# First attention of a two-layer block: head pairs on two halves of the array's rows, stacks sent through memory, small pieces of work between score rounds

## The chip, the cores and the metric

The kernel runs on one core of a Trainium2 chip. The metric is the device time of one execution in microseconds. A core has a matrix engine (PE, with weight loads shown as PEld), a vector engine (DVE), a scalar engine (ACT), a general engine (POOL), and a queue that issues transfers (SP). Each works through its own list in order and waits on semaphores for the others. PE works out of SBUF into PSUM banks of 512 fp32 columns.

## What is computed

The block takes x of 16 batches of 512 tokens of 128 features: layer norm, first attention times a gate made from a quantised FFN, residual, layer norm, second attention times a gate from a mixture of experts, residual. The change touches the first attention alone, which has 16 heads of 8 dimensions:

```python
Q = relu(x @ Wq + bq); K = relu(x @ Wk + bk); V = relu(x @ Wv + bv)   # x: [16, 512, 128]
scores = einsum('bqhd,bkhd->bhqk', Qh, Kh) / sqrt(8)
scores = where(key_mask == 0, NEG, scores)
scores = where(tril == 0, NEG, scores)
attn = softmax(scores) * query_mask
out = einsum('bhqk,bkhd->bqhd', attn, Vh) + x
return gamma * (out - mean) / sqrt(var + 1e-8) + beta
```

## The kernel before, in words

Five stages run one after another: `norm_exact`, `ffn`, `attention0` (the first attention), `attention1` (the second), `experts`. `attention0` treats a **unit** of one batch and 8 heads at a time, so there are 32 units and two make a batch. The loop `turns` runs over two batches (four units, `s` = 0 to 3); each engine has its own `turn` with the order of its work written out by hand.

**Exact scores from bf16.** Q and K are projected in fp32 on PE (`project`, L1070), and ACT writes them twice, fp32 (`F`, L879) and bf16 (`part`, L880). POOL's `split` (L815 to L817) makes the two remaining bf16 parts. For a head, six products of parts are summed at once by laying the parts under each other in the rows of the stacks `QS` and `KS`: 6 x 8 rows, a row with the key mask at 64 and three rows with the bf16 parts of the negated row maximum at 96 (`MROW`). A matmul on the stacks uses 96 rows for maxima and 99 for scores. SP fills the stacks from `part` with 12 transfers of 64 KB for Q (L730) and 12 for K (L730), one mask row for each half of the heads (L735) and three rows of maxima a unit (L740). Four sets of stacks are in use.

**Unit.** For each pair of heads there are four banks of maxima (`max_bank`, L1082 and L1084): Q as weights, K as moving columns, and an added block of -1e30 above the diagonal, with the 128 x 128 matrices `identb` and `far`. DVE reduces each bank pair (L948). All 16 banks of unit u+1 are made while unit u is scored; DVE then splits the maxima into three bf16 parts (`m_split`, L956 to L959), PE turns them (`turn_m`, L1136), ACT copies them out (L898) and SP puts them into `QS`. For each pair there are also five score banks (`score_bank`, L1095 with `add_far`, L624 or L627), keys on partitions, into two alternating PSUM banks `pST`; ACT takes the exponential of each bank (L887). `weigh` (L1123) multiplies by V, four heads on four column groups, in fp32; ACT copies the result (`o_evac`, L892), PE turns it back (`turn_o`, L1130) and DVE divides by the sums (`o_normal`, L984 to L989).

**What sets the order.** `both` mixes maximum banks into the five score banks of a pair:

```python
for k in range(5):
    for _ in range(-(-len(todo) // (5 - k))):
        max_bank(u + 1, *todo.pop(0), i1)
    score_bank(u, p, k, i)
    if k in after:
        after[k]()
```

Pairs 0 and 1 carry five maximum banks each, pair 2 six, pair 3 none. PE begins unit u after `m_put` (the maxima's rows have landed), and its first bank is a maximum bank that also needs the stacks. In even units SP issues the stacks of the next batch (`stacks_q`, `stacks_k`), then `m_rows`, then the second half of the K stacks. At the end of an even unit DVE runs `normalise` (L995 to L998) and then `v_evac` (L965 to L973, nine instructions: bias, ReLU, key mask, ones columns). At the end of an odd unit it runs `normalise_x1` (to L1009). POOL's `residual` (L838 to L841) stands between them.

`attention1`, which is not changed, already works on pairs of 64-row heads (L1646, L1653 for scores, L1663 for maxima) with one pair of score banks and an exponential of 1024 columns (L1456).

Of the kernel before, what the change touches and what calls it, by code (L numbers as in the profile page):

```python
# [629 lines left out]
def attention0(nc, NB, XN, G, KM, ident, identb, far, x, Wq, bq, Wk, bk, Wv, bv, gamma, beta, x1_d, mask_d):  # L630

# [10 lines left out]
    PARTS_Q = (0, 0, 0, 1, 1, 2)  # L642
    PARTS_K = (0, 1, 2, 0, 1, 0)
    MASK, MROW = 64, 96
    VC = DH + 1
    PER_D, PER_G = 112, 20
    STACK = 7 * 16
    with ExitStack() as c:
# [7 lines left out]
        rows = sb("rows", [P, 3, P])  # L656
        xst = sb("xn_staged", [P, TOK])
# [4 lines left out]
        QS = [sb(f"QS{i}", [P, UH, TOK], BF16) for i in range(4)]  # L662
        KS = [sb(f"KS{i}", [P, UH, TOK], BF16) for i in range(4)]
        V = [sb(f"V{i}", [P, TB, HEADS * VC + 32 - VC]) for i in range(2)]
        vtmp = sb("vtmp", [P, TB, P])
        PT = [sb(f"PT{i}", [P, 5, TOK]) for i in range(4)]
        MX = sb("max", [P, UH, TB])
        mrest = sb("mrest", [P, UH * TB])
        mp = sb("mparts", [P, 3, UH * TB], BF16)
        mT = sb("mT", [UH * TB, 3, P], BF16)  # L670
        OT = sb("OT", [P, TOK])
        den = sb("den", [P, TB, 4])
# [6 lines left out]
        pST = [ps(f"pST{i}", [P, TOK]) for i in range(2)]  # L679
# [5 lines left out]
        zeroed, ones_set, v_set = sem("k_zeroed"), sem("k_ones_set"), sem("v_set")  # L685
        q_zeroed, q_ones_set = sem("q_zeroed"), sem("q_ones_set")
# [8 lines left out]
        q_stacked, k_stacked = [sem(f"q_stacked{i}") for i in range(2)], [sem(f"k_stacked{i}") for i in range(2)]  # L695
# [8 lines left out]
        loads = 3 + 2 * 2 * DH + 3  # L704

        @block.sync
        def _(sp):
# [12 lines left out]
            sp.wait_ge(mask_made, 3)  # L720
            sp.dma_start(mask_d, part[0:NT, 1, 0, 0:P]).then_inc(mask_stored, 16)
            sp.wait_ge(mask_stored, 16)

# [4 lines left out]
            def stack(i0, half, n, S, order, stacked):  # L728
                for at, k in enumerate(order):
                    sp.dma_start(S[i0 + half][DH * at:DH * at + DH, :, :],  # L730
                                 part[64 * half:64 * half + 64, n, k, :]).then_inc(stacked[half], 16)

            def mask_row(b, i0, half):
                row = mask_d[bass.ds(b * TB, TB), :].rearrange("(o a t) p -> o a (t p)", o=1, a=1)
                sp.dma_start(KS[i0 + half][MASK:MASK + 1, :, :], row.to_broadcast([1, UH, TOK])).then_inc(k_stacked[half], 16)  # L735

            def m_rows(u, i):
                mT_in.wait(sp, u)
                for k in range(3):
                    sp.dma_start(QS[i][MROW + k:MROW + k + 1, :, :], mT[:, k, :]).then_inc(m_put, 16)  # L740

            def stacks_q(b, i0, last_reader=None):
                q_parts.wait(sp, b)
                if last_reader is not None:
                    st_ready.wait(sp, last_reader)
                for half in range(2):
                    stack(i0, half, 0, QS, PARTS_Q, q_stacked)

            def stacks_k(b, i0, half):
                k_parts.wait(sp, b)  # L750
                stack(i0, half, 1, KS, PARTS_K, k_stacked)
                mask_row(b, i0, half)

            stage(0)
            sp.wait_ge(q_ones_set, 2)
            sp.wait_ge(ones_set, 2)
            stacks_q(0, 0)
            stacks_k(0, 0, 0)
            stage(1)
            m_rows(0, 0)  # L760
            stacks_k(0, 0, 1)
# [8 lines left out]

            def turn(i, first, last):
                for s in range(4):
                    u, b = i * 4 + s, i * 2 + s // 2
                    prep = s % 2 == 0 and not (last and s == 2)
                    if s % 2 == 0 and not (first and s == 0):
                        load_x(b - 1)
                    if prep:
                        if first and s == 0:
                            sp.wait_ge(q_ones_set, 4)
                            sp.wait_ge(ones_set, 4)  # L780
                        stacks_q(b + 1, (s + 2) % 4, 20 * (u - 1) + 19)
                        stacks_k(b + 1, (s + 2) % 4, 0)
                    if not (last and s == 3):
                        m_rows(u + 1, (s + 1) % 4)
                    if prep:
                        stacks_k(b + 1, (s + 2) % 4, 1)
                    if s % 2 == 0 and not (first and s == 0):
                        store_x1(b - 1, (s // 2 + 1) % 2)
                    if s % 2 == 1 and not (last and s >= 1):
                        stage(b + 2)  # L790
# [6 lines left out]
        def _(g):  # L797
            def clear(i0):

                for S in KS[i0:i0 + 2]:  # L800
                    g.memset(S[:], 0.0).then_inc(zeroed, 1)
                g.wait_ge(zeroed, i0 + 2)
                for S in KS[i0:i0 + 2]:
                    g.memset(S[MROW:MROW + 3, :, :], 1.0).then_inc(ones_set, 1)
                g.wait_ge(ones_set, i0 + 2)

            clear(0)
            for t in V:
                g.memset(t[:], 0.0).then_inc(v_set, 1)
            g.wait_ge(v_set, 2)  # L810

            def split(step, b, n, filled, stacked, done):
# [7 lines left out]
            g.wait_ge(w_in, 16 * loads)  # L820

            for w, into in ((wq0, wq), (wk0, wk)):
                for half in range(2):
                    g.tensor_copy(into[:, 64 * half:64 * half + 64].rearrange("c (d h) -> c d h", h=UH),
                                  w[:, 64 * half:64 * half + 64].rearrange("c (h d) -> c d h", h=UH)).then_inc(w_ordered, 1)
            step = Steps(g, pool)
            split(step, 0, 0, q_in, q_stacked, q_parts)
            split(step, 0, 1, k_in, k_stacked, k_parts)
            clear(2)
            before = step.n  # L830

            def residual(step, b, parity):

# [9 lines left out]

            def turn(i, first, last):
# [4 lines left out]
                for s in (0, 2):  # L849
                    b = i * 2 + s // 2  # L850
                    if not (last and s == 2):
                        split(step, b + 1, 0, q_in, q_stacked, q_parts)
                        split(step, b + 1, 1, k_in, k_stacked, k_parts)
                    if not (first and s == 0):
# [1250 lines left out]
```

## Time and profile before

| | us |
|---|---|
| runs | 3512.64 median (3512.46, 3512.64, 3522.1) |
| profiled execution | 3512.28, its span 3510.6, mean granted clock 0.935 |
| PE busy in the span | 2817.1 (80%) |
| DVE busy | 2341.5 (67%) |
| ACT busy | 1521.8 (43%) |
| POOL busy | 1262.9 (36%) |

Times in the profile are microseconds from the span's start, unless marked ns. The granted clock is a share of TensorE's full 2.4 GHz, and it has two levels, 0.5 and 1.0; a value between them is a mean. Matmuls overlap, so the time that one costs is read from start to start and not from its length. In a row of the trace, "out<-in" names what is written and read, xN is how many were merged, and the brackets give the idle time of the engine before it and what ended that. "issue" there is a wait that the profile shows no releaser for.

### The profile page before, as it was taken

How to read it: one execution, taken by the hardware profiler on the slowest of the kernel's cores; microseconds unless marked ns; L12 is line 12 of the kernel's file. 1: busy time of each engine (PE TensorE's matmuls, PEld its weight loads, DVE VectorE, ACT ScalarE, POOL GpSimd, SP SyncE). 2: the span in 40 equal slices, each digit the busy share in tenths (PEclk: the TensorE clock that was granted, in tenths of full speed). 3: DMA queues.
4: the chain of work that ended last, by engine and by line, in shares of the span. 5: the costliest groups of instructions: out<-in, count | busy, mean ns of one | idle time of the engine just before them, and what ended most of it. 6: DMA issues, size and time to landing. Idle time of an engine off the chain costs nothing. (4 is left out here: it accounts for less than half of the span.)

```text
span 3510.6 us, 66700 instructions
## 1 busy us (share of the span) xinstructions
PE 2817.1 (80%) x21313; PEld 1947.4 (55%) x21313; DVE 2341.5 (67%) x5836; ACT 1521.8 (43%) x2623; POOL 1262.9 (36%) x1384
## 2 busy tenths in 40 slices
PE   0046367777777788499999999999999987999999
PEld 0024134444444444366666666666666656888888
DVE  8978657777776777466666666666666645555555
ACT  3434234454444455254555545555555532232232
POOL 4546602121211211155555555555555550000000
PEclk9986579998989899699999999999999998999999
DMA  1000123222221312101111111111111112010100
GB/s 48 0 6 0 25 30 47 39 44 35 41 45 36 51 35 32 37 28 35 34 34 34 34 34 34 34 34 34 34 34 34 32 35 64 24 36 24 34 26 24
DMA packets 152527, 116.24 MB, mean 33 GB/s; under 512 B 35506, under 2 KB 127155, under 8 KB 152372
## 3 DMA queue, kind: packets, MB, share of 16 engines
q1 hardware_dynamic: 152372, 114.25, 14.2%
q8 instruction: 87, 1.43, 0.2%
q14 instruction: 68, 0.56, 0.1%
HBM read 60.96 MB, written 17.32 MB: 22 GB/s over the span
## 5 line engine op out<-in xcount | busy, mean ns | idle before, releaser
L1539 DVE CUSTOM_DVE_ANT_0 a_scored<-a_pMax,a_causal 128x128 bf16<-128x128 f32 (+3 forms) x1024 | 449.7, 485 | 444.0 <-PE a_pMax L1663 444.0
L948 DVE TENSOR_REDUCE a_max<-a_pMax 128x2 f32<-128x256 f32 (+3 forms) x512 | 406.8, 822 | 209.3 <-PE a_pMax L1084 198.4
L887 ACT ACTIVATE a_PT<-a_pST 128x512 f32<-128x512 f32 x640 | 370.6, 597 | 403.3 <-PE a_pST L624 268.4
L1456 ACT ACTIVATE a_PT<-a_pST 128x1024 f32<-128x1024 f32 (+1 forms) x384 | 338.8, 882 | 361.2 <-PE a_pST L1653 349.8
L1082 PE MATMUL a_pMax<-a_KS,a_QS 96*128 96x128 bf16 (+3 forms) x1024 | 283.8, 329 | 203.3 <-DMA a_QS<-a_mT 134.6
L1405 POOL TENSOR_SCALAR_AFFINE_SELECT a_PT<-a_PT 128x256 f32<-128x256 f32 x512 | 203.0, 409 | 603.5 <-ACT a_PT L1456 573.0
L1942 ACT ACTIVATE m_silu<-m_pG 128x512 f32<-128x512 f32 x256 | 153.3, 599 | 410.2 <-PE m_pG L2034 410.2
L1671 PE MATMUL a_pO<-a_PT,a_V 128*64 128x512 f32 (+3 forms) x2048 | 307.3, 443 | 0.7 <-POOL a_PT L1405 0.7
L1082 PEld LDWEIGHTS a_pMax<-a_KS,a_QS 96*128 96x128 bf16 x1024 | 106.8, 105 | 309.4 <-issue 197.9
L1095 PE MATMUL a_pST<-a_QS,a_KS 99*128 99x512 bf16 (+3 forms) x1024 | 256.8, 315 | 16.4 <-ACT a_PT L887 14.4
L2042 PEld LDWEIGHTS m_pY<-m_w,m_hT 128*128 128x128 f32 x2048 | 248.0, 191 | 9.9
L815 POOL TENSOR_TENSOR a_rest<-a_qk,a_parts 128x512 f32<-128x512 f32 x32 | 37.0, 1155 | 593.9 <-ACT a_parts L880 593.7
L1989 DVE TENSOR_TENSOR m_hT<-m_pU,m_silu 128x512 f32<-128x512 f32 x256 | 177.0, 691 | 108.9 <-PE m_pU L2034 90.6
L2042 PE MATMUL m_pY<-m_w,m_hT 128*128 128x128 f32 x2048 | 248.8, 275 | 0.0
L1423 POOL TENSOR_TENSOR a_SM<-a_PT 128x768 f32<-128x768 f32 x128 | 235.0, 1836 | 10.6
L1671 PEld LDWEIGHTS a_pO<-a_PT,a_V 128*64 128x64 f32 x2048 | 136.6, 137 | 164.5 <-issue 145.3
L1910 POOL TENSOR_TENSOR m_out<-m_silu_acc,m_y 128x512 f32<-128x512 f32 x16 | 20.3, 1270 | 561.5 <-ACT m_silu_acc L1934 561.5
L1084 PE MATMUL a_pMax<-far,identb 128*128 128x128 bf16 x1024 | 221.9, 235 | 0.0
L2002 DVE SCALAR_TENSOR_TENSOR m_acc<-m_pY,m_cw,m_acc 128x128 f32<-128x128 f32 x448 | 126.3, 344 | 126.8 <-PE m_pY L2042 126.8
L1646 PE MATMUL a_pST<-a_q_high,a_k_high 64*128 64x512 f32 (+3 forms) x1024 | 198.9, 385 | 4.0 <-ACT a_PT L1456 4.0
L1653 PE MATMUL a_pST<-a_max_rows,a_ones_rows 64*128 64x512 f32 (+3 forms) x1024 | 151.8, 333 | 50.5 <-DMA a_max_rows<-a_mT 50.5
L1663 PE MATMUL a_pMax<-a_k_high,a_q_high 64*128 64x128 f32 (+3 forms) x1024 | 166.8, 363 | 8.0 <-DVE a_max L1539 6.6
(282 smaller groups left out, 6861.7 us busy)
## 6 DMA issues: line engine op xcount, KB each, us to landing
a_rden<-inverse_sums_dram SPq DMA_DIRECT2D x256, 128.0 KB, 2.9
a_QS<-a_parts SPq DMA_DIRECT2D x192, 64.0 KB
a_KS<-a_parts SPq DMA_DIRECT2D x192, 64.0 KB
a_xn_staged<-xn SPq DMA_DIRECT2D x32, 256.0 KB, 2.4
a_max_rows<-a_mT SPq DMA_DIRECT2D x512, 2.0 KB
ln_x<-in_L_attn_x SPq DMA_DIRECT2D x8, 512.0 KB, 7.2
a_x<-in_L_attn_x SPq DMA_DIRECT2D x16, 256.0 KB, 3.0
x_dram<-a_att SPq DMA_DIRECT2D x16, 256.0 KB, 3.8
```

The costliest lines, as they stand in the source:

```text
L887: a.activation(PT[p][:, k], pST[(5 * p + k) % 2][:], ACT.Exp, scale=SCALE).then_inc(exped.sem, 1)
L948: v.tensor_reduce(MX[:, 2 * p:2 * p + 2, j], pMax[j % 2][:, :, 0:(j + 1) * P], AX.X, ALU.max, negate=True).then_inc(maxed.sem, 1)
L1082: pe.matmul(pMax[j % 2][:, hh, 0:(j + 1) * P], QS[i][0:MROW, h, j * P:(j + 1) * P], KS[i][0:MROW, h, 0:(j + 1) * P], start=True, stop=False)
L1084: mm = pe.matmul(pMax[j % 2][:, hh, j * P:(j + 1) * P], identb[:], far[:], start=False, stop=True)
L1095: pe.matmul(bank[:, at:at + TOK - kb * P], KS[i][0:MROW + 3, h, kb * P:(kb + 1) * P], QS[i][0:MROW + 3, h, kb * P:TOK], start=(at == 0), s ...
L1405: g.affine_select(out=blocks, in_=blocks, compare_op=ALU.is_ge, fill=0.0, base=0, pattern=[[0, 2], [1, P]], channel_multiplier=-1).then_in ...
L1423: step.then(g.tensor_tensor(S[:, :, P:TOK], T[:, :, P:TOK], T[:, :, AT[1]:AT[1] + TOK - P], ALU.add))
L1456: a.activation(PT[s.q % 2][:, :, k * TOK:k * TOK + w], pST[:, :, 0:w], ACT.Exp, scale=SCALE).then_inc(exped.sem, 1)
L1539: last = v.tensor_tensor_reduce(scored[:, cc, at:at + w], pMax[:, cc, at:at + w], causal[:, TOK - w:], -1.0, 3e38, ALU.add, ALU.min, MX[pa ...
L1646: pe.matmul(pST[:, cc, at:at + w], K[i][rows, keys], Q[i][rows, queries], start=(n == 0 and at == 0), stop=False)
L1671: mm = pe.matmul(pO[DH * cc:DH * cc + DH, kb * P:TOK], V[pair // 2 % 2][:, kb, head:head + DH], PT[pair % 2][:, cc, AT[kb]:AT[kb] + TOK - ...
L2042: mm = pe.matmul(pY[e % 2][:, t], HT[HC * (e % 2) + k][:, t * P:(t + 1) * P], W2[:, e, k], start=(k == 0), stop=(k == HC - 1))
```

## The change

- **Pairs on row halves.** A pair is now head h of the first eight and head h of the second eight. One has rows 0 to 63 of the array, the other rows 64 to 127. The mask row moves to 48 and the maxima to 49 to 51 within each half, so there are two sets of stacks and not four. A unit is four such pairs.
- **Rounds.** A pair has three score rounds (1024, 1024 and 512 columns over both heads) into one pair of banks `pST`, and three maximum rounds into two alternating pairs of banks. Three exponentials replace five, 12 a unit.
- **Stacks through memory.** Q and K parts are written to DRAM (`put_q`, `put_k`, 3 and 4 transfers a batch), with copies made by repeated sources. From there each of two groups of four pairs is filled with four transfers of 4 KB rows (`stack`). The ones of the mask rows are set once. The three maxima's rows of both halves take 2 transfers a unit, not 3.
- **Ahead.** Maxima run 6 pairs ahead of scores (`LEAD`). Projections are made two batches ahead and put out in odd units, the values one batch ahead in even units.
- **Pieces.** PE's weighs, turns and projections, and DVE's layer norms, are cut into pieces and stand between the rounds. The values' evacuation goes from DVE (nine instructions) to ACT (one); the bias is added on PE by a one-row matmul, and the key mask is left to the scores. `turn_m` is one transpose and not three.

The core of the diff:

```diff
+    PAIRS, NS, NM, LEAD = 4, 3, 3, 6
+    AT = (0, TOK, 2 * TOK, TOK + 3 * P)
+    WIDTH = (TOK, TOK, 2 * P)
+    ROUNDS = (((0, 0),), ((0, 1), (3 * P, 3)), ((0, 2),))
+    MAXB = (((3, 0),), ((0, 0), (2, P)), ((1, 0),))
...
+            def put_parts(dst, n, groups, put):
+                for at, count, k, parts in groups:
+                    src = part[:, n, k:k + 1, :].to_broadcast([P, count, TOK]) if parts == 1 else part[:, n, k:k + count, :]
+                    sp.dma_start(dst[at:at + count].rearrange("a s d h t -> (s d h) a t"), src).then_inc(put, 16)
+            def put_q(b):
...
+                put_parts(qs_d, 0, ((0, 3, 0, 1), (3, 2, 1, 1), (5, 1, 2, 1)), q_put)
+            def put_k(b):
...
+                put_parts(ks_d, 1, ((0, 3, 0, 3), (3, 2, 0, 2), (5, 1, 0, 1)), k_put)
+                sp.dma_start(ks_d[NPART, :, 0], row.to_broadcast([2, UH, TOK])).then_inc(k_put, 16)
+            def stack(b, parity, group, last_score=None):
+                heads = slice(PAIRS * group, PAIRS * (group + 1))
+                if group == 0:
+                    sp.wait_ge(q_put, PUT_Q * (b + 1))
+                    sp.wait_ge(k_put, PUT_K * (b + 1))
+                if last_score is not None:
+                    st_ready.wait(sp, last_score)
+                for half in range(2):
+                    sp.dma_start(KS[parity][key_rows(half), heads, :],
+                                 ks_d[:, half, :, heads].rearrange("a d h t -> a d (h t)")).then_inc(k_stacked[group], 16)
+                for half in range(2):
+                    sp.dma_start(QS[parity][part_rows(half), heads, :],
+                                 qs_d[:, half, :, heads].rearrange("a d h t -> a d (h t)")).then_inc(q_stacked[group], 16)
...
+                    n = Unit(i, s, first, last)
+                    u, b = n.u, n.b
+                    if not n.odd:
+                        if n.values:
+                            stack(b + 1, 1 - n.parity, 0, NS * PAIRS * (u - 1) - 1)
+                            stack(b + 1, 1 - n.parity, 1, NS * PAIRS * u - 1)
+                        if not (last and s == 0) and not (last and s == 2):
+                            stage(b + 2)
+                        if not n.no_before:
+                            load_x(b - 1)
+                    elif not n.no_before:
+                        store_x1(b - 1, 1 - n.parity)
+                    if n.prepare:
+                        put_q(b + 2)
+                    if not n.end:
+                        m_rows(u + 1, (s + 1) % 4 // 2, (s + 1) % 2)
+                    if n.prepare:
+                        put_k(b + 2)
...
+            def v_evac(b, parity):
...
+                a.activation(heads[:, :, :, 0:DH], pM[:].rearrange("p (t h d) -> p t h d", t=TB, d=DH), ACT.Relu).then_inc(v_in.sem, 1)
+                at, w = k * TOK, WIDTH[k]
+                a.activation(PT[p][:, :, at:at + w], pST[:, :, 0:w], ACT.Exp, scale=SCALE).then_inc(exped.sem, 1)
...
+                    lead(0, 0)
+                    if not n.start:
+                        o_normal(step, 2 * u - 2, before_a[0], before_a[1], 0, before_a[2])
+                    lead(0, 1)
+                    lead(0, 2)
+                    layer_norm(0, True)
+                    lead(1, 0)
+                    layer_norm(1, True)
+                    lead(1, 1)
+                    layer_norm(2, True)
+                    lead(1, 2)
+                    if not n.end:
                         m_split(step, u + 1)
+                    layer_norm(3, True)
+                    lead(2, 0)
+                    if not n.start:
+                        o_normal(step, 2 * u - 1, before_a[0], before_a[1], 1, before_a[2])
+                    lead(2, 1)
+                    layer_norm(0, False)
+                    lead(2, 2)
+                    layer_norm(1, False)
+                    lead(3, 0)
+                    layer_norm(2, False)
+                    lead(3, 1)
+                    layer_norm(3, False)
+                    lead(3, 2)
...
+            def values(b, ts=(0, 1, 2, 3)):
+                for t in ts:
+                    into = pM[:, t * P:(t + 1) * P]
+                    pe.matmul(into, XT[:, t * P:(t + 1) * P], wv[:], start=True, stop=False)
+                    mm = pe.matmul(into, one[0:1, :], rows[0:1, 0, :], start=False, stop=True)
...
+            def max_round(u, par, pair, p, m):
+                n = NM * (PAIRS * u + p) + m
+                bank = pMax[(NM * p + m) % 2]
+                maxed.wait(pe, n - 2)
+                for k, (j, at) in enumerate(MAXB[m]):
+                    w = (j + 1) * P
+                    for half in range(2):
+                        pe.matmul(bank[:, half, at:at + w], QS[par][masked_rows(half), pair, j * P:(j + 1) * P],
+                                  KS[par][masked_rows(half), pair, 0:w], start=(k == 0), stop=False)
+                for half in range(2):
+                    mm = add_far(pe, bank[:, half], [at + j * P for j, at in MAXB[m]], identb, far)
                 mm.then_inc(max_ready.sem, 1)
...
+            def score_round(u, par, pair, p, k):
+                exped.wait(pe, NS * (PAIRS * u + p) + k - 1)
+                for at, kb in ROUNDS[k]:
+                    for half in range(2):
+                        rows = split_rows(half)
+                        pe.matmul(pST[:, half, at:at + TOK - kb * P], KS[par][rows, pair, kb * P:(kb + 1) * P],
+                                  QS[par][rows, pair, kb * P:TOK], start=(at == 0), stop=False)
+                for half in range(2):
+                    mm = add_far(pe, pST[:, half], [at for at, _ in ROUNDS[k]], far, identb)
+                mm.then_inc(st_ready.sem, 1)
...
+                    def scores(p, k):
+                        score_round(u, par, PAIRS * group + p, p, k)
+                        lead(p, k)
+                    def weigh_before(kbs):
+                        if not n.start:
+                            weigh(u - 1, 1, 1 - group, par if n.odd else 1 - par, kbs)
+                    pe.wait_ge(m_put, M_PUT * (u + 1))
+                    scores(0, 0)
+                    weigh_before((0,))
+                    scores(0, 1)
+                    weigh_before((1,) if n.prepare else (1, 2, 3))
+                    scores(0, 2)
+                    if not n.start:
+                        o_in.wait(pe, 2 * u - 2)
+                    else:
+                        mT_in.wait(pe, 0)
+                    if n.prepare:
+                        project(b + 2, wq, q_ready)
+                    scores(1, 0)
+                    if n.prepare:
+                        weigh_before((2, 3))
+                    if n.values:
+                        values(b + 1, (0, 1))
+                    scores(1, 1)
+                    if n.prepare:
+                        q_in.wait(pe, b + 2)
+                        project(b + 2, wk, k_ready)
+                    if n.values:
+                        values(b + 1, (2, 3))
+                    scores(1, 2)
+                    if n.lead(2, last) is not None:
+                        batch_stacked(b + 1, group)
+                    scores(2, 0)
+                    if n.prepare:
+                        k_in.wait(pe, b + 2)
+                    if n.values:
+                        v_in.wait(pe, b + 1)
+                    if not n.start:
                         turn_o(2 * u - 1)
+                    weigh(u, 0, group, par, (0,))
+                    scores(2, 1)
+                    weigh(u, 0, group, par, (1,))
+                    scores(2, 2)
+                    if not n.end:
+                        if not n.start:
+                            o_in.wait(pe, 2 * u - 1)
+                        turn_m(u + 1)
+                    scores(3, 0)
+                    weigh(u, 0, group, par, (2, 3))
+                    if n.turn_x:
                         mT_in.wait(pe, u + 1)
+                        turn_x(b + 2)
+                    scores(3, 1)
+                    scores(3, 2)
+                    if n.turn_x:
+                        xT_in.wait(pe, b + 2)
+                    elif n.end:
+                        o_in.wait(pe, 2 * u - 1)
+                    else:
+                        mT_in.wait(pe, u + 1)
+                    turn_o(2 * u)
```

## Rows read from the trace of the kernel before

**Rows 1.** Table of stages: us, busy time of PE, PEld, DVE, ACT, POOL; clock, DMA share, GB/s

```profile
462.00:1405.00 943.00, 723.55 (x6221) 419.16 (x6225) 680.62 (x1738) 457.49 (x808) 178.46 (x150) 0.91 0.25 40
```

**Rows 2.** Timeline of two units, SP queue and PE: start, length, what

```profile
878.05 1.86 SPq L740 DMA_DIRECT2D a_QS<-a_mT  x3
...
893.58 7.92 SPq L730 DMA_DIRECT2D a_QS<-a_parts  x12
...
906.44 2.97 SPq L740 DMA_DIRECT2D a_QS<-a_mT  x3
...
936.66 2.39 SPq L740 DMA_DIRECT2D a_QS<-a_mT  x3
...
914.98 0.29 PE L1082 MATMUL a_pMax<-a_KS,a_QS 96*128 96x128 bf16 x1 [7.04 <-DMA a_QS<-a_mT]
```

**Rows 3.** Groups by line, loop: count | busy us, mean ns | idle before, releasers

```profile
L1082 PE MATMUL a_pMax<-a_KS,a_QS 96*128 96x128 bf16 x992 | 271.1, 325 | 183.4 <-DMA a_QS<-a_mT 134.6 <-DVE a_max L948 37.7 <-DMA a_KS<-mask_dram 10.7
...
L948 DVE TENSOR_REDUCE a_max<-a_pMax 128x2 f32<-128x256 f32 x496 | 393.8, 822 | 200.3 <-PE a_pMax L1084 189.3 <-issue 3.3 <-DVE a_V L973 0.2
```

**Rows 4.** Timeline of DVE at the end of an even unit

```profile
903.68 0.69 DVE L995 TENSOR_TENSOR a_att<-a_att,xn 128x512 f32<-128x512 f32 x1 [0.35 <-DVE a_mparts L959]
...
908.94 0.68 DVE L965 TENSOR_TENSOR a_vtmp<-a_pM,a_rows 128x512 f32<-128x512 f32 x1
...
914.59 0.17 DVE L973 COPY a_V<-key_mask 128x16 f32 x1
```

**Rows 5.** Timeline of PE in the first attention

```profile
862.91 2.36 PE L1123 MATMUL a_pO<-a_PT,a_V 128*32 128x512 f32 x32
...
865.20 0.28 PE L1082 MATMUL a_pMax<-a_KS,a_QS 96*128 96x256 bf16 x1
...
870.76 0.60 PE L1130 MATMUL a_pM<-ident,a_OT 128*128 128x128 f32 x4
...
886.12 0.38 PE L1095 MATMUL a_pST<-a_QS,a_KS 99*128 99x384 bf16 x2
...
886.45 1.02 PE L1070 MATMUL a_pM<-a_xT,a_wq 128*128 128x512 f32 x2
...
887.30 0.22 PE L1082 MATMUL a_pMax<-a_KS,a_QS 96*128 96x128 bf16 x1
```

**Rows 6.** Timeline of PE in the second attention

```profile
2007.50 0.34 PE L1646 MATMUL a_pST<-a_q_low,a_k_high 64*128 64x384 f32 x2
...
2007.68 0.34 PE L1646 MATMUL a_pST<-a_q_high,a_k_low 64*128 64x384 f32 x2
...
2008.42 0.45 PE L1663 MATMUL a_pMax<-a_k_high,a_q_high 64*128 64x512 f32 x2
...
2008.80 0.28 PE L1685 MATMUL a_pM<-ident,a_mparts 128*16 128x128 f32 x1
...
2009.38 0.39 PE L1633 MATMUL a_pM<-a_xT_high,a_wqT_low 128*128 128x512 f32 x1
...
2009.71 0.39 PE L1646 MATMUL a_pST<-a_q_high,a_k_high 64*128 64x256 f32 x2
...
2009.93 0.28 PE L1646 MATMUL a_pST<-a_q_low,a_k_high 64*128 64x256 f32 x2
```

**Rows 7.** Timeline of ACT in the same stretch

```profile
2008.63 1.02 ACT L1456 ACTIVATE a_PT<-a_pST 128x1024 f32<-128x1024 f32 x1 [0.60 <-PE a_pST L1653]
...
2010.48 0.60 ACT L1456 ACTIVATE a_PT<-a_pST 128x512 f32<-128x512 f32 x1
```

**Rows 8.** Groups by line, loop: exponentials, bf16 evacuation of a projection

```profile
L887 ACT ACTIVATE a_PT<-a_pST 128x512 f32<-128x512 f32 x640 | 370.6, 597 | 403.3 <-PE a_pST L624 268.4 <-PE a_pST L627 126.9
...
L880 ACT ACTIVATE a_parts<-a_pM,a_bqk 128x512 bf16<-128x512 f32 x30 | 20.7, 689 | 0.0
```

**Rows 9.** Table of stages: the first loads of x, and the stacks of a batch

```profile
14.00:18.00 4.00, 0.00 (x0) 0.00 (x0) 3.62 (x13) 0.53 (x2) 0.00 (x0) 1.00 1.20 290
...
893.60:914.00 20.40, 12.17 (x111) 6.97 (x108) 18.24 (x50) 9.37 (x17) 7.88 (x7) 0.90 0.52 74
```

More of the change, by code:

```diff
@@ L842, in residual @@
                 g.sem_inc(x1_made.sem, 1)
+            step = Steps(g, pool)
+            for b in range(2):
+                split(step, b, 0, q_in, q_parts)
+                split(step, b, 1, k_in, k_parts)
+            before = step.n
+            tail = [None]
             def turn(i, first, last):
@@ L848, in turn @@
                     step.base = step.base - 4
[L849 to L854, printed above, removed]
-                        residual(step, b - 1, (s // 2 + 1) % 2)
+                for s in range(4):
+                    n = Unit(i, s, first, last)
+                    if n.prepare:
+                        split(step, n.b + 2, 0, q_in, q_parts)
+                    if n.prepare:
+                        split(step, n.b + 2, 1, k_in, k_parts)
+                    if not n.odd and not n.no_before:
+                        residual(step, n.b - 1, 1 - n.parity)
                 if first or last:
                     tail[0] = step
-            tail = [None]
             turns(g, COUNT, turn)
@@ new lines, in tile_stats, with variance @@
+            def tile_stats(step, A, eps):
+                for t in range(TB):
+                    last = v.bn_stats(stats[:, t], A[:, t])
+                step.then(last)
+                v.memset(t4[:], eps)
+            def variance(step):
+                for t in range(TB):
+                    last = v.bn_aggr(mv[:, t], stats[:, t])
+                step.then(last)
+                step.then(v.tensor_tensor(mv[:, :, 1], mv[:, :, 1], t4[:], ALU.add))
+                step.then(v.tensor_scalar(y4[:].bitcast(I32), mv[:, :, 1].bitcast(I32), -0.5, RSQRT_SEED, ALU.mult, ALU.add))
@@ L1045, in turn, with lead @@
-                    if s % 2 == 0 and not (last and s == 2):
-                        v_evac(step, b + 1, 1 - par)
-                    if s % 2 == 1 and not (first and s == 1):
-                        normalise_x1(step, b - 1, 1 - par)
+                    n = Unit(i, s, first, last)
+                    u, b = n.u, n.b
+                    before_a = (b, 0, n.parity) if n.odd else (b - 1, 1, 1 - n.parity)
+                    def lead(p, m):
+                        target = n.lead(p, last)
+                        if target is not None:
+                            maxima(target[0], target[2], m)
@@ new lines, in layer_norm @@
+                    def layer_norm(piece, odd):
+                        if n.odd == odd and not n.no_before:
+                            (normalise_x1 if odd else normalise)(step, b - 1, 1 - n.parity, piece)
+                    lead(0, 0)
[5 more added lines that the diff above has]
+                    lead(1, 0)
@@ L1201, in next_m @@
-                    def next_m():
-                        if more:
-                            if first and s == 0:
-                                k_in.wait(pe, b + 1)
-                            else:
-                                o_in.wait(pe, 2 * u - 1)
-                            turn_m(u + 1)
-                    pe.wait_ge(m_put, 48 * (u + 1))
-                    both(u, 0, s, range(0, 5) if more else [], i1, {0: o_first, 3: next_q})
-                    if not (first and s == 0):
-                        weigh(u - 1, 1, 1 - half, par if half else 1 - par)
```

552 lines of the change are left out of this document (256 added, 296 removed).

## Prediction

> **What bounds the kernel now.** I read the table of stages first: the first attention's loop fills 462 to 1405 us, with PE busy 723.6 of 943, DVE 680.6, ACT 457.5, DMA a quarter, granted clock 0.91 [rows 1]. No engine is full. The SP queue gives the rhythm: rows of maxima leave at 878.05, 906.44 and 936.66, so this batch of two units takes 58.6 us, a unit 29.3 [rows 2]; 32 units fill the 943 us at 29.5. In each batch SP issues the next batch's stacks from 893.58; the rows of maxima leave behind 18 of them at 906.44, and PE stands 7.04 us before its first maximum at 914.98 [rows 2]. The groups by line add it up: 134.6 us of PE's idle time for those rows and 37.7 for DVE's maxima, while DVE waits 189.3 us for PE's maxima [rows 3]. That DVE idles and is late in the same loop comes from piles: behind the even unit's maxima it runs normalise from 903.68 and the values' evacuation from 908.94 to 914.8, 11 us without a maximum [rows 4].
>
> **Columns and halves.** 768 bf16 columns (384 and 128, then 256) are issued from 886.12 to 886.45 [rows 5]: 0.43 ns a column. A pair's score and maximum products have 2 x 2 x 1280 columns, its `far` adds 2 x 1024; four pairs make 28,672 columns, 12.3 us a unit now, and 7.9 if the halves of a product run together. The second attention shows two 64-row matmuls of 384 columns in 0.18 us, 2007.50 to 2007.68 [rows 6]: together, though in fp32r. No row has 64-row bf16; I take the fp32r row, with no overlap (+4.4 us a unit) as the other end.
>
> **What it adds on PE: switches.** Products use 64 rows and `far` 128, and the new order is product, `far`, product, `far` in each of 12 rounds: 48 changes a unit, none of them there now. Going from 64 to 128 rows at 2008.42 takes 0.38 us for 512 columns (0.16 too much), from 128 to 64 at 2009.38 takes 0.33 (0.11 too much) [rows 6]. I take 0.14. Behind it the first fp32r product lasts 0.22 us for 256 columns, 0.11 more, for its weights [rows 6]; no row tells this for bf16, so the ends are 0.03 and 0.25, and 0.14 is the nearest. Rounds then cost PE 7.9 + 48 x 0.14 = 14.6 us a unit, more than the 12.3 of now: what the halves give is spent on changes.
>
> The Trainium skill, TensorEngine Tiling (Array Packing), Key Properties, says that changing the tiling mode drains TensorE; Theoretical Speedup there gives up to 2x for 64 rows. By the second alone the rounds would be 7.9 us, by both 14.6; the trace agrees with both, at 0.11 to 0.16 us a drain.
>
> **Pieces on PE, a unit.** Two weighs of 2.3 us (862.91 to 865.20) [rows 5], each cut in three with 0.14 at the sides: 5.5. Odd unit: two projections of 0.85 (886.45 to 887.30), two turns of O under 0.6, I take 0.45, one turn of the maxima 0.1 [rows 5]: 2.7. Even: turns 1.0, x 0.5, values 1.4 with the bias rows (an estimate from the turn and the projection): 2.9. PE's list is 22.8 us.
>
> **The round trip.** With one score pair of banks, scores and exponentials alternate. In the second attention the next matmul behind a score's last add goes at 2008.42 and the exp starts 0.21 later; it ends at 2009.65 and the next product starts 0.06 after it, at 2009.71; exps take 1.02 for 1024 columns and 0.60 for 512 [rows 6, 7]. Rounds: 0.06+0.22+0.14+0.11+0.21+1.03 = 1.77, then 1.88 and 1.23; a unit 19.5. During the exp PE makes its maximum round and a piece, so a round lasts the longer of the trip and PE's items, which are 1.22, 1.44 and 1.00 plus the piece. Odd unit, pair 0 with a weigh and project q: 2.27, 2.29, 1.85; pair 1 with a weigh and project k: 2.07, 2.29, 2.3 (there two evacuations of k of 0.69 [rows 8] stand ahead of the exp); pair 2 with a turn of O and a weigh: 2.72, 2.29, 1.23; pair 3: 2.07, 1.88, 1.45. Sum 24.7. Even: 2.27, 2.9, 1.23; 1.95, 2.2, 1.6; 2.72, 2.29, 1.23; 2.6, 1.88, 1.45, together 24.3.
>
> **DVE, ACT, POOL.** The maxima cost the same, 16 instructions of 0.822 [rows 3] (12 releases in place of 16). Of DVE's 680.6 us [rows 1] the values take 15 x 5.6 = 84 [rows 4]; the rest is 19.2 a unit for the 31 units in the window, with 0.2 for one more instruction in each O step and 1.2 for gaps between chained steps 20.6. It has cover under 24.5; for maxima that meet a layer-norm piece I add 0.5 us a unit. The values become one ACT instruction of some 0.7 us; ACT's exps are 4 x (1.03+1.03+0.60) = 10.6 us for 20 x 0.597 = 11.9 now [rows 8], with evacuations 14: covered. If that cover went (PE at 20 us) ACT still would not bind. POOL has the same instructions; its residual must end before DVE's first piece in the odd unit, 6 us behind normalise: covered.
>
> **SP and memory.** The maxima of unit u+1 are complete in the middle of u, and their rows leave by 17 us of 25: the wait of [rows 2] is gone. What is late next is the stack. Ahead of put_k stand the store of x1, put_q and the rows of maxima; put_k leaves at 18 to 22 us of the odd unit. It writes 0.79 MB in 1 KB pieces: 11 us at the 74 GB/s of the present stacks, 2.7 at the 290 of the first loads [rows 9]; I take 4. It lands 3 us into the even unit, group 0 (0.85 MB) leaves by 6 and is needed before pair 2, at 12.3. It moves in 4 KB rows, for which the loads at 290 are nearest: 2.9 us, landed by 11 with the receipt, no wait; the other end is 11.5, a wait of 7 us a batch.
>
> **Ends.** Before the loop a second batch is projected and six more maximum rounds run, while half of the stacks need clearing: 0, ends -5 and +10. The last one and a half units have no maximum rounds: -5. The tail's chain stays.
>
> **Sum.** (24.7 + 24.3)/2 + 0.5 = 25.0 a unit; 32 x 25.0 - 5 = 795 us for 943. That is -148 on the profiled execution's 3512.3 us (span 3510.6; median of the runs 3512.6): **3364 us**.
>
> **Rivals.**
> - *The forecast*: PE's list with its changes and the round trip, 24 to 26.5 us a unit: 3335 to 3415. Chance 0.57.
> - *DVE is the bound*: bf16 changes are nearly free (the priced rows are fp32r), the round trips shrink, and DVE's 20.6 stands with 1.4 of waits: 22.0 us, 704 in all, 3273. Chance 0.17.
> - *The stacks are late*: 3 to 7 us in 15 batches are 45 to 105, so 3410 to 3470, with a lower clock behind each stop. For it: the present stacks hold half the engines (share 0.52) at 74 GB/s [rows 9]. Against: those are 1 KB pieces. Chance 0.15.
> - *Slower*: the halves don't overlap in bf16 and a change costs 0.22. Rounds cost PE 12.3 + 10.6 = 22.9, with pieces 31.1, with trips that it can't hide 31.5: 32 x 31.5 - 5 = 1003, 3573 us. It decides from 29.6 us a unit. Against it: the overlap in [rows 6]. Chance 0.08.
> - *No change*: half of the above, changes at 0.22 with some overlap lost, meets the lost wait. Chance 0.03.
>
> The Trainium skill, DMA: Bandwidth & Descriptors, "How many engines (k)", lets a transfer use only as many engines as divide its slowest dimension: 7 of 16 for a K stack, 6 for Q. By that rule a group takes about 6.5 us and lands just in time; the share of 0.52 with targets of 8 rows agrees.
>
> **Numbers.** 3364 us. The range of 3270 to 3470 takes in the second and third case and the bounds on changes and stacks; one in five is left out. A difference under 0.3% can't be told from none here: faster 0.89, same 0.03, slower 0.08.
>
> **What would show it.** Units 24 to 26 us apart; two 64-row bf16 products of 512 columns in 0.22 us, and 0.11 to 0.16 lost at every `far`; no PE wait over 2 us; PE busy over 85% of the loop, granted clock 1.00. Wrong: a wait of PE for the stack before pair 2; DVE busy over 90%; a granted clock of 0.5 (1.2 GHz) in the loop; a second half that starts when the first has ended.

## The result, and the profile after

Six executions of the changed kernel took 3474.64 to 3503.1 us, median 3484.93; six of the kernel before 3511.8 to 3522.1, median 3515.01. The ratio is 0.9911, with a 95% interval of 0.9885 to 0.9937: faster by some 30 us, under 1%. The forecast was 148. The profiled execution of after took 3474.64 us (span 3472.6), against 3512.28 (3510.6) before.

Where the 38.0 us between the two spans lie is read from the exponentials' first and last start (the view of one line's instructions: shortest, median and longest in ns, then first and last start). L887 and L1456 are the exponentials of the first and the second attention before, L939 and L1561 those after:

```profile
L887 ACT ACTIVATE a_PT<-a_pST x640: 579/597/617, 463.7 to 1404.6; 128x512 f32<-128x512 f32 x160
...
L1456 ACT ACTIVATE a_PT<-a_pST x384: 597/1023/1029, 1478.8 to 2879.6; 128x1024 f32<-128x1024 f32 x128, 128x512 f32<-128x512 f32 x64
```
```profile
L939 ACT ACTIVATE a_PT<-a_pST x384: 588/1023/1036, 458.2 to 1331.3; 128x1024 f32<-128x1024 f32 x128, 128x512 f32<-128x512 f32 x64
...
L1561 ACT ACTIVATE a_PT<-a_pST x384: 597/1023/1030, 1402.7 to 2842.2; 128x1024 f32<-128x1024 f32 x128, 128x512 f32<-128x512 f32 x64
```

The first attention goes from 940.9 to 873.1 us (a unit from 29.4 to 27.3), what lies ahead of it and between the attentions gains 8.3, what follows 0.6, and the **second attention, whose code is unchanged, goes from 1400.8 to 1439.5 us**. So two things are to be explained: a gain of half of what was forecast, and a loss of 38.7 us in a place that the change doesn't touch.

The stage table of after, beside [rows 1]:

```profile
460.00:1330.00 870.00, 767.87 (x6131) 301.55 (x6129) 640.43 (x1657) 422.64 (x561) 171.94 (x144) 0.87 0.22 69
```

PE is now busy for 88% (77% before), but the granted clock is 0.87, lower than the 0.91 of before. TensorE's timeline shows what the forecast took for the halves and the changes of rows:

```profile
852.78 0.39 PE L1192 MATMUL a_pST<-a_QS,a_KS 64*128 64x512 bf16 x2 [0.49 <-ACT a_PT L939]
853.11 0.29 PE L624 MATMUL a_pST<-identb,far 128*128 128x128 bf16 x2
853.33 0.39 PE L1181 MATMUL a_pMax<-a_KS,a_QS 49*128 49x512 bf16 x2
853.65 0.29 PE L624 MATMUL a_pMax<-far,identb 128*128 128x128 bf16 x2
...
846.98 0.44 PE L1169 MATMUL a_pM<-a_wv,a_xT 128*128 128x128 f32 x2
847.35 0.48 PE L1170 MATMUL a_pM<-a_rows,a_one 1*128 1x128 f32 x2
...
831.86 0.40 PE L1181 MATMUL a_pMax<-a_KS,a_QS 49*128 49x256 bf16 x2 [2.40 <-DVE a_max L1005]
```

From one start to the next, two bf16 products of 512 columns take 0.33 us: 0.22 for one set of columns (at the prediction's 0.43 ns a column), so the halves do overlap, and 0.11 for the change to 128 rows. Two `far` products take 0.22: 0.11 for their own columns, and again 0.11 for the change back. The last row is one that no step foresaw: PE stands 2.40 us for a maximum of DVE. It lies in the odd unit; what DVE and POOL do ahead of it is in their timelines of the same stretch:

```profile
818.72 1.23 DVE L1005 TENSOR_REDUCE a_max<-a_pMax 128x2 f32<-128x1024 f32 x1
...
820.46 1.08 DVE L1045 TENSOR_SCALAR a_y<-a_mv 128x4 int32<-128x4 int32 x1
821.67 1.29 DVE L1005 TENSOR_REDUCE a_max<-a_pMax 128x2 f32<-128x256 f32 x2
822.87 0.15 DVE L1049 SCALAR_TENSOR_TENSOR a_t<-a_y 128x4 f32<-128x4 f32 x1
823.06 1.05 DVE L1050 TENSOR_TENSOR a_t<-a_t,a_mv 128x4 f32<-128x4 f32 x1
824.14 1.09 DVE L1051 SCALAR_TENSOR_TENSOR a_y<-a_t,a_y 128x4 f32<-128x4 f32 x1
825.26 0.16 DVE L1049 SCALAR_TENSOR_TENSOR a_t<-a_y 128x4 f32<-128x4 f32 x1
825.46 1.01 DVE L1050 TENSOR_TENSOR a_t<-a_t,a_mv 128x4 f32<-128x4 f32 x1
826.50 0.16 DVE L1051 SCALAR_TENSOR_TENSOR a_y<-a_t,a_y 128x4 f32<-128x4 f32 x1
```
```profile
820.37 1.15 POOL L863 TENSOR_TENSOR a_parts<-a_qk,a_parts 128x512 bf16<-128x512 f32 x1
...
822.93 1.16 POOL L862 TENSOR_TENSOR a_rest<-a_qk,a_parts 128x512 f32<-128x512 f32 x1 [0.18 <-POOL a_parts L864]
824.04 1.17 POOL L863 TENSOR_TENSOR a_parts<-a_qk,a_parts 128x512 bf16<-128x512 f32 x1
825.29 1.16 POOL L864 TENSOR_TENSOR a_parts<-a_rest,a_parts 128x512 bf16<-128x512 f32 x1
```

Operations on 4 elements a partition, which take 0.16 us when POOL rests, take 1.01 to 1.09 here, and each ends 0.02 us after one of POOL's splits: 821.54 behind 821.52, 824.11 behind 824.09, 825.23 behind 825.21, 826.47 behind 826.45. The reductions of L1005, which read PSUM, run on beside POOL. The Trainium skill, Trainium Architecture — The Big Picture, What this means for kernel authors, calls the pair of ports that DVE and GpSimd share an exclusive lock and not a split of bandwidth; the four ends agree. Four such stalls are 3.6 us more on DVE in this batch. PE's waits for DVE's maxima, 1.82 us at 827.53 and 2.40 us at 831.86, and behind them the clock, in the table of the same stretch (columns as in [rows 1]):

```profile
827.53 0.39 PE L1181 MATMUL a_pMax<-a_KS,a_QS 49*128 49x128 bf16 x4 [1.82 <-DVE a_max L1005]
...
820.00:830.00 10.00, 6.50 (x54) 2.23 (x52) 8.67 (x24) 4.86 (x8) 6.11 (x6) 1.00 0.24 79
830.00:840.00 10.00, 7.52 (x55) 2.87 (x55) 7.41 (x16) 3.59 (x6) 0.00 (x0) 0.66 0.25 83
```

In the second attention a wait of VectorE (after, 1402 to 2842 us; before has none of the kind) and queue 14, which fetches the engines' code, differ. Its rows are for 1500 to 2700 us, before and then after (packets, MB, share):

```profile
DVE a_max L1644 <- issue: 12.3, 13, 1.3
```
```profile
q14 instruction: 7, 0.06, 0.0%
```
```profile
q14 instruction: 68, 0.56, 0.2%
```

In that stretch the kernel before fetches code 7 times on queue 14, the kernel after 68 times, five pieces of 8 KB in each turn of the loop (two at 1669, then 1672, 1675 and 1716, and again 91 us later), and VectorE stands about 1 us for code in a turn. These stalls, 12.3 us, are not the whole loss: PE's waits for the rows of the maxima grow from 50.5 to 65.4 us, and the granted clock of the stage is 0.98 (1.00 before). In the compiled stream (64 bytes an instruction) VectorE's loop of the second attention has 267 instructions in both kernels; before it starts at instruction 1587, after at 1515, since the first attention has 72 instructions fewer. In pieces of 128 instructions (8 KB) that is 51 and 107 into a piece.

### The profile page after: what moved, and what is told of

Same layout as the page of the kernel before. It is cut to its first block and busy times, and to the rows that moved or that the text cites. A ratio compares the mean times of both kernels' runs of the same rounds, so it can differ in the third digit from the quotient of the medians.

```text
span 3472.6 us, 65333 instructions
## 1 busy us (share of the span) xinstructions
PE 2886.7 (83%) x21249; PEld 1834.7 (53%) x21249; DVE 2281.3 (66%) x5750; ACT 1491.3 (43%) x2383; POOL 1242.1 (36%) x1379
## 3 DMA queue, kind: packets, MB, share of 16 engines
q14 instruction: 126, 1.02, 0.1%
## 5 line engine op out<-in xcount | busy, mean ns | idle before, releaser
L1005 DVE TENSOR_REDUCE a_max<-a_pMax 128x2 f32<-128x1024 f32 (+3 forms) x512 | 403.4, 820 | 217.9 <-PE a_pMax L624 115.1
L939 ACT ACTIVATE a_PT<-a_pST 128x1024 f32<-128x1024 f32 (+1 forms) x384 | 338.6, 882 | 385.2 <-PE a_pST L624 239.9
L1561 ACT ACTIVATE a_PT<-a_pST 128x1024 f32<-128x1024 f32 (+1 forms) x384 | 338.9, 882 | 380.9 <-PE a_pST L1758 366.6
L1776 PE MATMUL a_pO<-a_PT,a_V 128*64 128x512 f32 (+3 forms) x2048 | 324.7, 462 | 0.7 <-POOL a_PT L1510 0.7
L872 POOL TENSOR_TENSOR a_att<-a_att,a_rows 128x512 f32<-128x512 f32 x16 | 20.2, 1264 | 643.4 <-DVE a_att L1066 643.4
L1181 PE MATMUL a_pMax<-a_KS,a_QS 49*128 49x512 bf16 (+3 forms) x1024 | 152.2, 337 | 55.0 <-DVE a_max L1005 46.5
L1206 PE MATMUL a_pO<-a_PT,a_V 128*32 128x512 f32 (+3 forms) x2048 | 196.8, 491 | 0.2 <-ACT a_PT L939 0.2
L1192 PE MATMUL a_pST<-a_QS,a_KS 64*128 64x512 bf16 (+3 forms) x1024 | 149.7, 331 | 52.5 <-ACT a_PT L939 48.3
L1571 ACT COPY a_o<-a_pO 128x512 f32<-128x512 f32 x128 | 74.9, 585 | 224.8 <-PE a_pO L1776 224.8
```

What stands on the lines that cost most here:

```text
L939: a.activation(PT[p][:, :, at:at + w], pST[:, :, 0:w], ACT.Exp, scale=SCALE).then_inc(exped.sem, 1)
L1005: last = v.tensor_reduce(MX[:, :, p, j], pMax[(NM * p + m) % 2][:, :, at:at + (j + 1) * P], AX.X, ALU.max, negate=True)
L1206: mm = pe.matmul(pO[32 * cc:32 * cc + 32, kb * P:TOK], V[par][:, kb, VC * h:VC * h + 32], PT[p][:, half, AT[kb]:AT[kb] + TOK - kb * P], st ...
L1561: a.activation(PT[s.q % 2][:, :, k * TOK:k * TOK + w], pST[:, :, 0:w], ACT.Exp, scale=SCALE).then_inc(exped.sem, 1)
L1776: mm = pe.matmul(pO[DH * cc:DH * cc + DH, kb * P:TOK], V[pair // 2 % 2][:, kb, head:head + DH], PT[pair % 2][:, cc, AT[kb]:AT[kb] + TOK - ...
```

## The experiments

Every group of runs has its own executions of the kernel before, with medians of 3519.56 us (e1 to e4), 3516.58 (e5 to e8) and 3515.76 (e9 and e10); the ratios are to these. All runs from e3 on keep e1's writes (72 in e3, 71 from e4 on), so the second attention stays at 1403 to 1410 us in them, and what follows is about the first.

**Where the code lies.** e1: the kernel after, e2: the kernel before, each with short writes of VectorE ahead of the second attention.

```
 # attention1, vector block           (e1; e2 has 56)
+for n in range(72):
+    v.memset(pad[:, n:n + 1], 0.0)
 v.wait_ge(ones_set, 2)
```

> The changed kernel, with 72 one-column writes of VectorE put ahead of the second attention's setup (in a stretch in which VectorE is idle for 11.9 us), so that VectorE's loop of the second attention begins at instruction 1587 of its stream, as in the kernel before, and not at 1515. Nothing else differs. Theory 1 (code placement: in the profile after, VectorE fetches code in every turn of the second attention's loop, 5 times 8 KB, and stands 12.3 us in 13 stalls; before, none): the fetches and stalls go, the second attention falls from 1439.5 to about 1401 us between its first and last exp, its clock dips go, total 3435 to 3455. Theory 2 (the placement doesn't matter; the second attention is slower because its data or its transfers lie otherwise, or by chance of that execution): within 0.3% of 3485, or 4 us more for the 72 writes.

> The kernel before, with 56 one-column writes of VectorE at the same place, so that its loop of the second attention begins at instruction 1643, which is 107 past a multiple of 128, as in the kernel after (1515). Theory 1 (code placement): 4 or 5 fetches in each turn of the loop and a VectorE stall of about 1 us per turn, the second attention goes from 1400.8 to about 1439 us, total 3545 to 3555. Theory 2: 3515 as before.

Measured: e1 3450.56 us, ratio to before 0.9815 (0.9778 to 0.9852); e2 3545.15, 1.0074 (1.0057 to 1.0091). The second attention took 1408.3 us in e1 and 1434.8 in e2 (1439.5 and 1400.8 in the kernels that they are made from). Queue 14 from 1500 to 2700 us, e1 and then e2:

```profile
q14 instruction: 5, 0.04, 0.0%
```
```profile
q14 instruction: 67, 0.55, 0.1%
```

Nearly all of the loss of 38.7 us is shown to be a matter of where a loop begins: it goes with the place (31.2 us of it go in e1), and comes with it into the kernel before as well (34.0 in e2). The Trainium skill, Advanced Engine Details and Errata, ISA Cache, gives 32 KB in two lines of 256 instructions. By that e2's loop (1643 to 1909, in lines 6 and 7) would have stayed resident; the rows show 67 fetches, so the measurement decides. A guess that would fit both pairs is that three pieces of 128 stay and four don't; counted from the first instruction all three placements touch three, so this isn't shown, and neither is at which offset between 51 and 107 it tips. e1 keeps 7.5 us over the kernel before in this stage, and the later runs 2.6 to 9.2; that stays open.

**POOL beside DVE.** e3 shrinks POOL's splits to 8 of their 512 columns, so that the bf16 parts of the later batches are left out; e4 moves the second layer norm's pieces to the next even unit, one batch later, and computes the same.

```
 # e3, gpsimd, in the loop (and rest[:, 0:w] and so on in split)
-split(step, n.b + 2, 0, q_in, q_parts)
+split(step, n.b + 2, 0, q_in, q_parts, 8)
 # e4, vector, layer_norm
-if n.odd == odd and not n.no_before:
-    (normalise_x1 if odd else normalise)(step, b - 1, 1 - n.parity, piece)
+if x1 and not n.odd and not first:
+    normalise_x1(step, b - 2, n.parity, piece)
+if not x1 and not n.odd and not n.no_before:
+    normalise(step, b - 1, 1 - n.parity, piece)
```

> As e1_pad_after, and in the loop of the first attention GpSimd's splits of the projections work on 8 of 512 columns (the parts of the later batches are left stale). Theory A (VectorE's small operations with two inputs stand about 1 us each behind GpSimd's tensor operations in the odd unit, four times a batch, and the waits of TensorE of 1.8 and 2.4 us behind them drop the clock to 1.2 GHz): the means of L1050, L1051 and L1045 fall to 0.17 us, the batch from 54.6 to 51 us or less, total 3390 to 3425. Theory B (the unit is set by TensorE's own list, the stalls are hidden): within 10 us of e1_pad_after.

> As e1_pad_after (71 writes, the loop of the second attention again at 1587), and the second layer norm of a batch is moved from the odd unit, where its pieces lie beside GpSimd's splits, to the first two pairs of the next even unit, one batch later. The same computation. Theory A: the four stalls a batch of about 1 us go, VectorE's list of the odd unit falls from about 23 to 18 us, TensorE's waits for the maxima of the odd unit go, total 3395 to 3430. Theory B: within 10 us of e1_pad_after. Rival C: the even unit, now with both layer norms, becomes VectorE's own bound at some 26 us, and the gain is given back: 3435 to 3460.

Measured: e3 3392.08 us, 0.9643 (0.9624 to 0.9661); e4 **3372.95 us, 0.9581 (0.9561 to 0.96)**, the best of the versions that compute the same up to here. L1050 by line in the stretch of the loop, after and then e4 (shortest, median, longest in ns):

```profile
L1050 DVE TENSOR_TENSOR a_t<-a_t,a_mv x90: 161/164/1144, 533.8 to 1315.5; 128x4 f32<-128x4 f32 x90
```
```profile
L1050 DVE TENSOR_TENSOR a_t<-a_t,a_mv x87: 161/163/164, 532.8 to 1237.4; 128x4 f32<-128x4 f32 x87
```

In both the stalls go and the time falls, as theory A has it (e3 in its range, e4 22 us below it); B would have had them at 3450, C at 3435 or more. The first attention takes 824.2 us in e3 and 804.1 in e4, 25.8 and 25.1 us a unit for 27.5 in e1. The stage table of e4:

```profile
460.00:1262.00 802.00, 721.53 (x6137) 294.53 (x6137) 618.41 (x1632) 423.31 (x562) 172.09 (x144) 0.94 0.24 75
```

The clock is 0.94, above the 0.91 of [rows 1]. The four stalls took 3.6 us of DVE in the batch shown, 3.1 a batch in the mean of the loop. e3, which takes away the stalls (and much of POOL's work), gives 3.4 us a batch (2 x 27.47 less 2 x 25.76), e4 4.7 (2 x 27.47 less 2 x 25.13): PE was behind the stalls in full. Its waits for the maxima fall from 42.6 us in e1 to 12.1 in e3 and 10.5 in e4, and its clock rises from 0.87 to 0.92 and 0.94. That e4 beats e3 was not foreseen; e4 also empties the odd unit of DVE's pieces, and what that alone is worth was not measured.

**Halves and changes of rows**, on e4:

```
 # e5: both halves read the rows of half 0 (masked_rows(0), split_rows(0))
 # e6, add_far: the mask's product contracts over its own half's rows, the other half of the mask is left out
-return pe.matmul(bank[...], lhsT[:], rhs[:], start=False, stop=True)
+return pe.matmul(bank[...], lhsT[rows, :], rhs[rows, :], start=False, stop=True)
```

> As e4_x1_norm_moved, but both products of a pair in the first attention's score and maxima rounds read the rows of half 0, so they can't run beside each other (the heads of half 1 get the scores of half 0; instructions and columns are the same). Theory (the halves overlap, and that carries most of the change's gain): 1280 columns a pair for the scores and as many for the maxima are paid twice, 0.53 us by 8 per unit or 4.3 us, of which TensorE's present waits absorb some; unit 25.3 to between 28.5 and 29.6 us, total 3475 to 3510, so near the kernel before. Rival (the gain comes from the waits that went, not from the overlap): within 20 us of 3373.

> As e4_x1_norm_moved, but the causal mask's product of each half contracts over the 64 rows of that half only (the other half of the mask's rows is left out), so no product over 128 rows stands between those over 64. Theory (a change from 64 to 128 rows and back costs TensorE 0.10 to 0.11 us each, 48 a unit, about 5 us): TensorE's list falls from about 22 to 17 us a unit, VectorE's 20.8 us are next, unit 25.3 to 22.5 to 23.5, total 3285 to 3320. Rival (the 0.2 us ahead of these weight loads is a wait that would be there anyway, or exp's round trips set the unit): within 15 us of 3373.

e5: 3601.0 us, 1.0224 (1.02 to 1.0248). The direction is the theory's, the size beyond it: 228 us over e4 where 137 were the most. Two products of 512 now take 0.54 from start to start where they took 0.33, as expected; the rest is the clock:

```profile
460.00:1480.00 1020.00, 983.07 (x6039) 368.77 (x6041) 617.00 (x1632) 418.15 (x550) 172.74 (x144) 0.79 0.19 59
...
852.35 0.60 PE L1196 MATMUL a_pST<-a_QS,a_KS 64*128 64x512 bf16 x2
852.89 0.29 PE L624 MATMUL a_pST<-identb,far 128*128 128x128 bf16 x2
```

PE's list of 22.6 us a unit (721.53 over 31.9 units) and 4.3 more are 26.9 at a clock of 0.94, and 32.0 at 0.79; measured 32.5. PE was busy for 96% of it and the clock was still down (880 to 890 us: busy for all of the 10 us, at 0.51), so idle time alone doesn't explain every fall; why it stayed low here is open.

e6: 3332.71 us, 0.9477 (0.9461 to 0.9493), 40 us under e4 and not the 53 to 88 of the theory, but well beyond its rival. A round of 512 columns:

```profile
855.99 0.39 PE L1196 MATMUL a_pST<-a_QS,a_KS 64*128 64x512 bf16 x2 [0.34 <-ACT a_PT L939]
856.22 0.22 PE L624 MATMUL a_pST<-identb,far 64*128 64x128 bf16 x2
856.27 0.38 PE L1185 MATMUL a_pMax<-a_KS,a_QS 49*128 49x512 bf16 x2
```

0.23 and 0.05 for 0.33 and 0.22: the two changes are gone, 0.21 us for each score and each maximum round, and the `far` products overlap too, another 0.06, so that this run measures both together. The unit fell by 1.5 us only (25.1 to 23.7): DVE is now busy 81% of the stage, PE waits 31.4 us for its maxima (10.5 in e4), 77.3 for exponentials (55.8) and 9.7 for the stacks (none in e4), and the clock is 0.90.

**The other terms**, on e4. e7 leaves out the values' bias, e8 makes the weighted sums in one piece and not in two to four, e9 adds the bias by one wide product, and e10 turns the maxima at the end of the unit:

```
 # e7: without pe.matmul(into, one[0:1, :], rows[0:1, 0, :], ...)
 # e8: weigh_before((0, 1, 2, 3)) behind scores(0, 0); weigh(u, 0, ..., (0, 1, 2, 3)) behind scores(2, 0)
 # e9: one product of one row by 4 x 128 columns ahead of the four tiles
 # e10: turn_m(u + 1), m_evac(u + 1) behind scores(3, 2), exp(u, 3, 2)
```

> As e4_x1_norm_moved, without the four one-row products a batch that add the values' bias (the bias is left out). If TensorE's list sets the even unit too, the 1.6 us a batch that they take come off: 3345 to 3352. If VectorE sets the even unit, which now has both layer norms: 3365 to 3375.

> As e4_x1_norm_moved, with the weighted sums of a group of pairs made in one piece, as in the kernel before, and not in two to four pieces between score rounds. Each piece of about 2.8 us then stands between two score rounds and holds up one exp; by TensorE's list it saves four changes of the rows used, about 0.5 us a unit. If the pieces are worth it (exp and maxima wait for them): 3385 to 3430. If the list alone counts: 3355 to 3370.

> As e4_x1_norm_moved, but the values' bias of a batch is added by one product of one row with 512 columns ahead of the four tiles, instead of four of 128. Leaving the four out gave 21 us. If the one costs what its columns cost (four passes, about 0.9 us against 1.6 us a batch), half of that comes: 3355 to 3366. If the one-row product's cost is all columns, nothing: 3370 to 3376.

> As e4_x1_norm_moved, but TensorE turns the maxima of the next unit at the end of the unit and ScalarE evacuates them there, no longer before the last pair: the maxima rows again have nothing to hide behind, as in the kernel before. If that wait was worth its length (transposition, evacuation and transfer are about 2.5 to 3 us after the last score round, 31 times, and the clock falls behind it): total 3455 to 3485. If other work of the unit's end takes it in: 3375 to 3400.

e7: 3352.32 us, 0.9529 (0.9512 to 0.9545), 21 us under e4 and at the edge of what was expected if PE's list sets the even unit: it does. e9: 3366.29 us, 0.957 (0.9549 to 0.959), 7 us under e4 with overlapping intervals, so not separated from it; what it computes is the same, and it has the lowest median of such versions. Its one product of 512 columns takes 1.05 us from start to start (812.32 to 813.37), four of 128 take 1.64. e8: 3454.73 us (3417.61 to 3471.41), 0.9777 (0.9702 to 0.9852); its first attention takes 872.1 us, 68.0 over e4's, so the pieces are worth more than expected. A whole sum (2.36 and 2.90 us in its timeline) holds up the next exp, and ScalarE's waits for L627, the round behind the first sum, grow from 147.3 us to 256.4, with the clock at 0.91. e10: 3535.8 us, 1.0054 (1.0032 to 1.0075), 163 us over e4 where 82 to 112 were expected, and slower than the kernel before: the wait for the maxima's rows is back, and the clock is 0.83. The rows are of e9, e8 and e10:

```profile
812.32 1.12 PE L1172 MATMUL a_pM<-a_rows,a_one 1*128 1x512 f32 x2
813.37 0.71 PE L1175 MATMUL a_pM<-a_wv,a_xT 128*128 128x128 f32 x4
...
846.12 2.36 PE L1210 MATMUL a_pO<-a_PT,a_V 128*32 128x512 f32 x32
...
PE a_pST L1196 <- DMA a_QS<-a_mT: 71.5, 29, 3.2
...
460.00:1420.00 960.00, 803.17 (x6086) 303.30 (x6085) 631.31 (x1633) 418.57 (x556) 171.74 (x144) 0.83 0.20 63
```

e10's stage is 158 us longer than e4's: PE stands idle 76 us more (156.8 for 80.5) and is busy 82 us longer (803.2 for 721.5) with the same products, at the lower clock.

## Why the prediction was wrong, and where it was right

It gave 3364 us (3270 to 3470) and 0.89 for faster; measured were 3484.93 and faster. Two of its steps failed, and both are shown by runs that take the effect away.

1. **"POOL has the same instructions ... covered."** The step counted POOL's instructions and DVE's, each by its own list, and never laid them over each other. In the kernel before the same operation (L72 there) never met a split (164 ns in the median, 165 at the longest, so the durations taken from there were those without POOL). The change puts the x1 norm's pieces between the maxima of the odd unit, where POOL splits. Four stalls a batch, PE's waits of 1.82 and 2.40 us, and a clock of 0.87: 27.3 us a unit for the forecast 25.0. Without the stalls (e3) the unit is 25.8; with the pieces elsewhere (e4) it is 25.1, and the first attention 804.1 us, 136.8 less than before.
2. **"That is -148 on the profiled execution's 3512.3 us"**, with nothing for the rest of the program. The change shortens VectorE's stream by 72 instructions ahead of the second attention's loop, and that loop no longer stays resident: +38.7 us in the profiled execution; e1 takes back 34 in the medians (31.2 in the stage).

Together: e4 stands 146.6 us under its own executions of before (3519.56 less 3372.95), next to the forecast's 148. So near a number is in part luck: the profiled executions differ by 134.3 only (3510.6 less 3376.3), and the terms below were off both ways.

- **PE's list**: forecast 22.8 us, 22.6 in e4. Its terms were off both ways, as the next two show.
- **Changes of rows**: forecast 0.14, measured 0.10 to 0.11 in bf16, 1.4 to 1.9 us a unit too dear. The fp32r rows [rows 6] had priced them too high, as the second rival held; DVE was still not the bound.
- **Values with bias rows**: forecast 1.4 us, measured 3.2 (0.37 and 0.41 for each of the four tiles; the trace has two entries for one fp32 product): 0.9 us a unit too cheap. A product of one row costs as much as one of 128.
- **Halves** overlap in bf16, 0.22 us for 2 x 512 columns: right, and e5 shows what it carries. The rival "slower" had 3573 for no overlap and a change of 0.22; e5, without overlap and with 0.11, is at 3601, since its clock is 0.79.
- **Round trip of the maxima**: right; no wait of PE for their rows is left, and e10 shows what its return costs with the clock, 163 us.
- **Stacks**: right. They leave at 839.56 to 845.8 us and PE has no wait for them in the loop, though that stretch moves 154 GB/s (840 to 850 us, DMA share 0.51) where the forecast took 290; in e6, with a unit of 23.7, PE does wait for them.
- **DVE's list**: forecast 20.6, measured 19.4 in e4 (618.41 over 31.9 units).
- **Granted clock 1.00**: wrong, 0.87, and 0.94 even in e4. "No PE wait over 2 us" was the right thing to look for: 2.40.

## What to carry to other kernels

When work is cut into pieces and moved between others, lay the timelines of VectorE and GpSimd over each other at the new place: here small VectorE operations out of SBUF (one input in L1045, two in L1050 and L1051) cost 0.16 us alone and up to 1.09 beside a GpSimd operation that they had to wait out, and equal lists say nothing of that. When a change alters the number of instructions of an engine, look at every later loop that nobody touched: count its code fetches in the trace, and move it by some unneeded instructions if it fetches in each turn (34 us here, for 72 one-column writes in a stretch in which the engine was idle). And price a wait of PE with the clock that follows it: in e10 71.5 us of waits for the maxima's rows came with 82 us of longer busy time.

## What the runs showed of the hardware that was not expected

- VectorE's L1045, L1050 and L1051 end 0.02 us behind GpSimd's running tensor operation, 0.85 to 0.93 us late; L1005, reading PSUM, isn't held.
- A loop of 267 VectorE instructions is fetched anew in every turn (67 or 68 pieces of 8 KB in 1200 us) or hardly at all (5 or 7), by where it begins; the stage is 31 to 34 us longer with the fetches.
- A one-row fp32 product of 128 columns takes 0.41 us from start to start, no less than one of 128 rows (0.37).
- Without overlap of the halves (e5) PE is busy for 96% of the stage and the granted clock is 0.79, lower than in any run with more idle time.
